# Which engine waits for the last scattered results: SyncE before, GpSimd now

## The reference, cut to what matters

```python
h = gelu(einsum('bfi,oi->bfo', x, W) + fc_bias + z + b)      # z: rank 16 side product
logits = h @ router_weight
topk_w, topk_i = top_k(logits, 2); topk_w = softmax(topk_w)
gate, up = (h @ gate_up_proj[e] + bias)[..., ::2], [..., 1::2]
act = (clip(up, -7, 7) + 1) * min(gate, 7) * sigmoid(1.702 * gate)
out = x + sum over the token's two experts of topk_w * (act @ down_proj[e] + down_bias[e])
```

## Time and profile before

| | us |
|---|---|
| median of 3 runs | 165.13 |
| lowest and highest of them | 162.73, 166.59 |
| the profiled execution's own time | 161.16 |
| its span, first to last instruction | 159.4 |
| TensorE's mean granted clock in it | 0.879 of full |
| busy: PE, DVE, ACT, POOL | 132.1, 97.5, 72.7, 97.5 |

### The profile page before, as it was taken

The page is one execution under the profiler, slowest core; times in us unless marked ns, Lnnn a source line. Parts: engine busy times, 40 slices in busy tenths (PEclk is TensorE's granted clock), DMA queues, the critical chain, the costliest instruction groups (busy, mean ns, idle before and its releaser), DMA issues.

```text
span 159.4 us, 3351 instructions
## 1 busy us (share of the span) xinstructions
PE 132.1 (83%) x933; PEld 115.6 (73%) x933; DVE 97.5 (61%) x308; ACT 72.7 (46%) x140; POOL 97.5 (61%) x138
## 2 busy tenths in 40 slices
PE   5994999996596499949999999999999999956300
PEld 5773776763572268939999999999999999945200
DVE  0418597965490595636456656575656679967930
ACT  3367688936460012133455464645555564341200
POOL 7889478778477267712256664666556665827720
PEclk9999999999758555796999999999999999996555
DMA  4989999912239208897696645625522994593740
GB/s 95 296 274 409 394 386 356 335 70 99 70 89 275 102 33 248 239 293 254 171 276 221 199 141 179 198 65 164 163 69 50 302 355 150 150 381 129 238 158 0
DMA packets 20000, 32.18 MB, mean 202 GB/s; under 512 B 4490, under 2 KB 12654, under 8 KB 19984
## 3 DMA queue, kind: packets, MB, share of 16 engines
q1 hardware_dynamic: 12736, 19.34, 38.4%
q0 software_dynamic: 3792, 8.43, 14.9%
q10 hardware_dynamic: 3456, 4.21, 8.4%
HBM read 19.14 MB, written 14.73 MB: 212 GB/s over the span
## 4 chain that ended last, share of the span: by engine, by line
PE 57%; DVE 20%; issue 8%; another core or an unknown queue 4%; DMA 3%; ACT 1%; ACTq 1%; SPq 1%; DVEq 0%
PE bank L969 17%; PE bank L990 8%; DVE x_sb L1264 6%; PE bank L956 5%; PE bank L810 4%; PE bank L820 3%; PE bank L964 3%; DMA x_sb<-in_x 3%; PE bank L978 3%; PE bank L986 3%; PE bank L786 2%; PE bank L742 2%; PE bank L831 2%; PE bank L800 2%
## 5 line engine op out<-in xcount | busy, mean ns | idle before, releaser
L571 POOL DMA_INDIRECT pair_results<-res,idx x47 | 47.3, 1007 | 37.0 <-issue 16.0
L562 POOL DMA_INDIRECT dispatched<-yrow,slot x32 | 36.4, 1137 | 16.2 <-issue 10.8
L674 ACT ACTIVATE ygT_hi<-bank 128x512 fp32r<-128x512 f32 (+1 forms) x24 | 14.1, 589 | 31.0 <-PE bank L956 29.1
L969 PE MATMUL bank<-wgu_hi,ygT_hi 128*128 x94 | 27.5, 293 | 0.0
L969 PE MATMUL bank<-wgu_raw,ygT_hi 128*128 x94 | 27.5, 292 | 0.0
L969 PE MATMUL bank<-wgu_hi,ygT_lo 128*128 x94 | 27.4, 291 | 0.0
L1229 DVE TENSOR_TENSOR ygT_lo<-bank,ygT_hi 128x512 fp32r<-128x512 f32 (+1 forms) x24 | 16.3, 680 | 12.1 <-issue 7.8
L1250 DVE TENSOR_SCALAR room<-bank 128x256 f32<-128x256 f32 (+1 forms) x24 | 10.0, 418 | 16.4 <-ACT room L686 12.0
L686 ACT ACTIVATE room<-bank 128x256 f32<-128x256 f32 (+1 forms) x24 | 9.1, 380 | 22.1 <-PE bank L969 15.3
L969 PEld LDWEIGHTS bank<-wgu_hi,ygT_hi 128*128 128x128 f32 x94 | 19.1, 204 | 0.0
L969 PEld LDWEIGHTS bank<-wgu_raw,ygT_hi 128*128 128x128 f32 x94 | 19.0, 202 | 0.0
(11 more groups left out here) (203 smaller groups left out, 266.5 us busy)
## 6 DMA issues: line engine op xcount, KB each, us to landing
wgu_raw<-in_L_ffn_gate_up_proj SPq DMA_DIRECT2D x8, 512.0 KB, 7.0
yg<-dispatched SPq DMA_DIRECT2D x31, 129.0 KB
yrow<-pair_results SPq DMA_DIRECT2D x6, 512.0 KB
dispatched<-pad SPq DMA_DIRECT2D x17, 129.0 KB
yg<-dispatched ACTq DMA_DIRECT2D x16, 129.0 KB
x_sb<-in_x SPq DMA_DIRECT2D x4, 512.0 KB, 5.1
wd_raw<-in_L_ffn_down_proj SPq DMA_DIRECT2D x4, 512.0 KB
out<-x_sb ACTq DMA_DIRECT2D x8, 256.0 KB
```

Source lines behind the costliest of these rows:

```text
L562: nc.gpsimd.indirect_dma_start(out=xs, out_offset=bass.IndirectOffsetOnAxis(ap=slot[:, t, k:k + 1], axis=0), in_=yrow[:, t, :], in_offset= ...
L571: nc.gpsimd.indirect_dma_start(out=rs, out_offset=bass.IndirectOffsetOnAxis(ap=idx[:, n:n + 1], axis=0), in_=res[:, n % RES, :], in_offset ...
L674: nc.scalar.activation(ygT["hi"][:, b, 0:n], ygT_ps[b][:, 0:n], ACT.Copy).then_inc(s_yhi, 1)
L969: last = nc.tensor.matmul(gu_ps[p % 2][:, j, :], ygT[yp][:, p % 2, j, c, :], wgu[wp][:, bass.ds(e * (HC * F2) + c * F2, F2)], start=False, ...
```

## The change

The loop over the eight `s_stored` semaphores is taken from the end of SP's body and put at the end of POOL's body, behind the loop of scatters. The values are the same: together they stand for all 47 scatters. Nothing else is changed.

```diff
@@ end of the body of SyncE @@
             results_stored(2)
             sp.wait_ge(s_sum, GT)
             read_back(3, (1,))
-            for u in range(STORES):
-                sp.wait_ge(s_stored[u], 16 * len(range(u, NB, STORES)))
 
@@ end of the body of GpSimd @@
                         in_=res[:, n % RES, :], in_offset=None,
                         bounds_check=last_row, oob_is_err=False).then_inc(s_stored[n % STORES], 16)
+
+            for u in range(STORES):
+                pool.wait_ge(s_stored[u], 16 * len(range(u, NB, STORES)))
```

## The result

| | before | changed |
|---|---|---|
| median of 5 runs, us | 166.59 | 169.93 |
| lowest and highest | 162.73, 172.21 | 167.12, 174.78 |
| profiled execution, us | 161.16 | 174.78 |
| its span | 159.4 | 172.9 |
| ratio, 95% interval | | 1.032 (1.024 to 1.041) |

The forecast was 166.9 us in a range of 161.5 to 168.8, 1.1% slower. The measured time lies above the range and the ratio is about three times the forecast; the two medians lie 2.0% apart. Two more runs of the kernel before, 171.62 and 172.21 us, lie outside what its first three had shown.

A forecast was written before the change was run, and what follows sets the result against it. The prediction took POOL's last DRAIN to set the kernel's end. Starting it 1.74 us later at unchanged 6.54 us length, added to the 165.13 us median, gave 166.9 us, range 161.5 to 168.8.

The forecast's parts named there:

- (a): End of SP's body: losing its eight waits is worth nothing, since POOL arrives last; cover 4.8 us.
- (b): End of POOL's body: eight added waits cost a few tens of ns each, shadowed by the landing except the last.
- (c): POOL's last DRAIN: its work starts at 154.4 instead of 152.66, 1.74 us later.
- (d): POOL's last DRAIN, behind the new waits: it takes 6.54 us and ends at 160.9.
- one transfer settled after another: POOL's last DRAIN: settles 79 transfers in issue order, 83 ns each, from when it starts; likeliest case, chance 0.53.
- short behind the waits: POOL's last DRAIN: long only from transfers in flight, then 0.1 us; 161.6 us, 2.1% faster; chance 0.21.
- count from the last landing: POOL's last DRAIN: a fixed 5.0 us tail from the last landing; 165.1 to 165.3 us; chance 0.15.
- work before the engine was free: POOL's last DRAIN: work began at record opening, up to 9.05 us; 169.4 us, 2.6% slower; chance 0.08.
- (e): Whole kernel: span 159.4 + 1.74 = 161.1; the same step on median 165.13 gives 166.9 us, 1.1% slower.

The follow-up runs named there:

- a kernel with an unchanged end: Kernel before with SyncE's eight waits for the scatters removed and none added on GpSimd; median 168.26 us, ratio 1.019 (1.007 to 1.030).
- one whose end is 2.6 us shorter: Kernel before with one more GpSimd DRAIN, ahead of the scatters of results; median 168.96 us, ratio 1.037 (1.027 to 1.047).

## Why the prediction was wrong

**(a) SyncE's waits are worth nothing:** right. With and without them the tail is 6.77 us, and 8.55 with them beside GpSimd's.

**(b) and (c), a wait on POOL costs only the later start of the DRAIN, 1.74 us:** right, 1.8 us in the first profile and 154.5 - 152.73 = 1.8 in the second; 1.5 and 2.15 in the other two, as the last landing came.

**(d) the DRAIN behind the waits takes 6.54 us:** right, 6.525 in each of the five profiles in which a DRAIN stands behind GpSimd's waits. The reading behind it, that the length goes with the number of transfers issued and not with their state, is borne out for 79 and 47 transfers. The picture of one transfer settled after another, with the landings never showing, was not: behind 32 and 15 transfers the DRAIN waited for the last landing and then took half of the 83 ns for each of them. With two such halves, and a wait for the last landing between them, the forecast for 79 would have been the same, since 3.3 us of work outlast the 1.4 us to the landing. GpSimd's 6,525 ns behind landed transfers decide against the rule in the Trainium skill's page "VectorE: DVE Perf Modes", section "The DRAIN you can't avoid", of about 12 ns on all five engines; SP's and ACT's 7 and 8 ns agree with it (SP's took 128 ns in the changed kernel).

**The rivals** fell: the DRAIN was not short behind the waits; it did not count from the last landing (the end moved by 1.8 us, and 2.8 us instead of 5.1 were left behind the landing where 47 transfers stood before it); and it did not work before the engine was free.

**(e) The sum is where it failed.** It put 1.74 us on a median of 165.13 us and took the spread around it, 2.4 under and 1.5 over, from three executions. The kernel before has executions from 159.5 to 174.6 us; the median of 54 is 170.2 and their mean 169.1. Base and range were mis-sized, not the step. Of the 4.8 us from 165.13 to the measured 169.93, 1.8 are the DRAIN, 1.5 came when two more runs of the kernel before moved its own median to 166.59, and the other 1.5 lie inside the spread. The 23 executions of the changed kernel have a mean of 171.0: 1.9 us more, 95% interval -0.1 to 3.7, with 1.8 us as the trace has it in the middle; the four differences within a set average 2.3. The first comparison's 3.2% overstates it, as far as can be told: such a ratio rests on a few executions, and the same procedure gave 1.9% for a kernel with an unchanged end and 3.7% for one whose end is 2.6 us shorter.

What is not shown: that the change leaves the body alone in every respect. The interval leaves room for up to 2 us that the change might add by making the limp more frequent: three of its four profiles limp, and one of two of the kernel before, which is too few to tell. Against it stands only that the kernel before, compared with itself, came out 3.0 us apart in mean, as far as any of the four comparisons of the changed kernel (2.6, 2.2, 3.0 and 1.4 us).

The warning was in the numbers of before: the profiled execution took 161.16 us, below all three timed runs, and I took that as a remark instead of a sign of a spread wider than the runs showed.

## What to carry to other kernels

Read the block's end as a list of arrivals: the chain of waits stopped at 153 us, and the 6 us behind it were one instruction that no busy time counts. A DRAIN of GpSimd is to be paid for every indirect transfer since the last one, and it can do a part of this while the last ones are still landing. A wait for the landings ahead of it takes that away and moves the end by as long as it holds the DRAIN back (1.5 to 2.15 us here). It can be shortened by an earlier DRAIN where GpSimd is idle and the transfers have landed, though neither kernel that had one here was faster; or left out if every landing is waited for elsewhere, which took 1.7 to 4.3 us off the mean in the three runs of it here. And where a profiled execution lies outside the timed runs, get the spread from more executions before writing a range.

## What the runs showed of the hardware

A DRAIN of GpSimd takes 83 ns for each indirect transfer issued since its last DRAIN: 6.53 us for 79 and 3.9 for 47. Behind 32 and 15 it waited for the last landing and took 1.35 and 0.65 us more, 0.042 us each. With no transfer before it, it took 0.2 us. The opening of its record can lie 3.4 us ahead of the engine's being free (151.5 against 154.95).

Eleven executions of one unchanged program on one chip spread from 159.5 to 173.3 us. Its two profiles show two rhythms of the same loop, 3.25 and 3.8 us for a pair of blocks, both at a granted clock of 1.00.
